# Windowed attention beside a ternary feed-forward layer: maxima as rows of the head stacks, masks in row groups of their own, three products a stack, two value buffers, new orders

## What is computed

```python
xn  = layernorm(x)
q, k, v = heads(xn @ Wq), heads(xn @ Wk), heads(xn @ Wv)     # 16 heads of 16
attn = softmax(q . k_window * 16**-0.5)     # a token sees itself and the 63 tokens before it
ctx = attn . v_window
h   = layernorm(gelu(xn @ ternary(W_fc).T), ln_w, ln_b)      # 1024 hidden features
out = x + ctx @ Wo + h @ ternary(W_proj).T
```

## Time and profile before

| what | value |
|---|---|
| median of three runs | 462.16 us |
| lowest and highest run | 457.6 and 462.68 us |
| the profiled execution, its own time | 454.42 us |
| its span, first to last instruction | 452.5 us |
| mean granted TensorE clock | 0.97 |

### The profile page before, as it was taken

One profiled execution on the slowest core, in us unless ns is written; L12 is line 12 of the kernel. 1 busy time (PEld: TensorE's weight loads), 2 busy tenths in 40 slices (PEclk: granted clock), 3 DMA queues, 4 the chain that ended last, 5 costly groups with the idle time before them and its releaser, 6 DMA issues.

```text
span 452.5 us, 13186 instructions
## 1 busy us (share of the span) xinstructions
PE 406.4 (90%) x5644; PEld 272.1 (60%) x5644; DVE 334.1 (74%) x693; ACT 309.1 (68%) x393; POOL 182.4 (40%) x112
## 2 busy tenths in 40 slices
PE   0396889799998999899998999999998999899894
PEld 0344554468646875578565874678465864677573
DVE  1885697559787887689767887689767975688664
ACT  2464278739677968877786758877786867796381
POOL 6200034245323644256305544255405731355572
PEclk9999799969999999999997999999999999999899
DMA  8759037800495046801691037801692029602001
GB/s 282 194 71 115 2 91 101 89 3 14 116 128 62 1 113 116 88 15 35 142 126 27 12 105 119 89 8 48 129 123 31 26 58 133 67 3 68 15 14 59
DMA packets 35226, 34.41 MB, mean 76 GB/s; under 512 B 5152, under 2 KB 33824, under 8 KB 35168
## 3 DMA queue, kind: packets, MB, share of 16 engines
q1 hardware_dynamic: 35168, 33.56, 44.7%
HBM read 7.35 MB, written 4.19 MB: 26 GB/s over the span
## 4 chain that ended last, share of the span: by engine, by line
PE 58%; DMA 14%; SPq 12%; DVE 7%; issue 4%; ACT 2%; POOL 2%; POOLq 0%
DMA k_stack<-qk_split 13%; SPq L324 11%; PE small L1114 8%; PE small L1103 7%; PE big L1093 6%; PE big L1021 6%; PE big L1081 5%; PE big L1033 4%; PE big L1066 4%; PE big L1060 4%; PE big L1086 3%; PE big L1047 3%; PE small L1130 2%; DMA x_in<-in_x 2%; PE big L1009 2%
## 5 line engine op out<-in xcount | busy, mean ns | idle before, releaser
L436 POOL TENSOR_TENSOR p_parts<-probs,p_parts 128x1024 f16<-128x1024 f32 x64 | 138.2, 2163 | 194.6 <-ACT p_parts L559 194.6
L558 ACT ACTIVATE probs<-big,exp_scale 128x1024 f32<-128x1024 f32 x64 | 71.4, 1115 | 53.3 <-PE big L1086 53.2
L738 DVE TENSOR_REDUCE negmax<-big 128x8 f32<-128x1024 f32 x64 | 78.1, 1222 | 23.0 <-PE big L1066 21.2
L559 ACT ACTIVATE p_parts<-big,exp_scale 128x1024 f16<-128x1024 f32 x64 | 71.3, 1114 | 0.0
L1103 PE MATMUL small<-proj_t,g_hi 128*128 128x256 f16 x256 | 60.8, 283 | 0.0
L1103 PE MATMUL small<-proj_t,g_lo 128*128 128x256 f16 x256 | 60.4, 282 | 0.0
L573 ACT ACTIVATE g_hi<-big,lnw_s 128x512 f16<-128x512 f32 x64 | 40.4, 689 | 25.5 <-PE big L1093 25.5
L1047 PE MATMUL big<-fc_t,xt_hi 128*128 128x512 f16 x128 | 48.7, 380 | 0.0
L1047 PE MATMUL big<-fc_t,xt_lo 128*128 128x512 f16 x128 | 48.5, 379 | 0.0
L732 DVE SCALAR_TENSOR_TENSOR g_lo<-big,lnw_s,g_hi 128x512 f16<-128x512 f32 x64 | 45.3, 739 | 2.4 <-ACT g_hi L573 2.1
L536 ACT ACTIVATE gel<-big 128x1024 f32<-128x1024 f32 x32 | 32.7, 1022 | 13.2 <-PE big L1047 12.8
(11 more groups left out here) (130 smaller groups left out, 786.4 us busy)
## 6 DMA issues: line engine op xcount, KB each, us to landing
q_stack<-qk_split SPq DMA_DIRECT2D x64, 128.0 KB, 4.3
k_stack<-qk_split SPq DMA_DIRECT2D x64, 128.0 KB, 7.3
x_in<-in_x SPq DMA_DIRECT2D x8, 512.0 KB, 4.8
out<-y_bufs SPq DMA_DIRECT2D x32, 128.0 KB, 1.7
v_odd<-v_even SPq DMA_DIRECT2D x16, 132.0 KB, 2.7
v_odd<-v_even SPq DMA_DIRECT2D x16, 99.0 KB, 2.2
y_bufs<-in_w_proj SPq DMA_DIRECT2D x1, 1024.0 KB, 5.5
gel<-in_w_fc SPq DMA_DIRECT2D x1, 1024.0 KB, 7.7
```

Of the source, the lines that this page charges most:

```text
L436: g.tensor_tensor(p_lo[:, j % PB], probs[:, j % PB], p_hi[:, j % PB], ALU.subtract).then_inc(*sig(p_lo_ready))
L558: s.activation(probs[:, j % PB].rearrange("p i (u q) -> p u i q", u=2), st, ACT.Exp, scale=exp_scale[:, 0:1]).then_inc(*sig(exp_ready))
L559: s.activation(p_hi[:, j % PB].rearrange("p i (u q) -> p u i q", u=2), st, ACT.Exp, scale=exp_scale[:, 0:1]).then_inc(*sig(p_hi_ready))
L738: v.tensor_reduce(negmax[:, j], slot[b, "sa", j][:].rearrange("p a (u k) -> p (a u) k", k=P), AX.X, ALU.max, negate=True).then_inc(*sig(ma ...
```

## The change

- Each stack has three products of 16 rows (lo·lo goes), so 12 DMAs a batch in place of 16. The two rows after them hold the split negated maxima, divided by 256, in `q_stack`, and 256 in `k_stack`. `fill_stacks` on DVE writes 256 over all of `k_stack` and zeros over its padding, ahead of `statistics(0)`; on POOL the zeros of `k_stack` go.
- `st` starts with two mask matmuls of 64 rows, one in each row group (`mask_k` is copied to partitions 64 to 127), its head matmuls have 50 rows, and those of `sa` 48. `shift`, `fill_shift` and `load_shift` go.
- `mt` is one job of four fp32 matmuls after all eight `sa`; `load_maxima` issues four DMAs of one row each.
- The values have two buffers; `v_upper` waits for the `pv` of two batches before.
- New lists for PE, ACT, DVE, POOL and SP: all eight `sa` of a batch stand ahead of its `gt`, `mt` and `st`, and x is loaded in the period in which its statistics are made. The first loads stand in another order.

```diff
-        v_even = sb("v_even", [P, 2, NT, NP, VC], fp16)
-        v_odd = sb("v_odd", [P, 2, NT, NP, VC], fp16)
+        v_even = sb("v_even", [P, 2, 2, NT, NP, VC], fp16)
+        v_odd = sb("v_odd", [P, 2, 2, NT, NP, VC], fp16)
...
-        negmax = sb("negmax", [P, NJ, NP], fp32)
-        mt = sb("mt", [4 * NP, 2, 2, P], bf16)
-        shift = sb("shift", [W + 2, NJ, NP * P], bf16)
+        negmax = sb("negmax", [P, NP, NJ], fp32)
+        mt = sb("mt", [P, 2, W], fp16)
...
-        PERIOD = [(-1, "pv", 6), (0, "gt", 3), (0, "mt", 0), (0, "v", 0), (-1, "pv", 7), (1, "xt", 0), (0, "sa", 4),
-                  (0, "proj", 0), (0, "st", 0), (1, "qk", 0), (-1, "ct", 1), (0, "st", 1), (1, "fc", 0), (0, "sa", 5),
-                  (-1, "wo", 1), (1, "qk", 1), (0, "sa", 6), (1, "fc", 1), (0, "pv", 0), (1, "fc", 2), (0, "sa", 7),
-                  (1, "fc", 3), (0, "st", 2), (0, "mt", 1), (0, "proj", 1), (0, "proj", 2), (0, "st", 3), (-1, "wo", 2),
-                  (1, "sa", 0), (0, "pv", 1), (1, "sa", 1), (0, "pv", 2), (0, "st", 4), (1, "sa", 2), (0, "st", 5),
-                  (0, "proj", 3), (0, "pv", 3), (1, "gt", 0), (0, "st", 6), (0, "pv", 4), (0, "ct", 0), (1, "sa", 3),
-                  (1, "gt", 1), (0, "st", 7), (0, "pv", 5), (-1, "wo", 3), (1, "gt", 2), (0, "wo", 0)]
-        ORDER = FIRST + [(p + ahead, kind, n) for p in range(NB + 1) for ahead, kind, n in PERIOD if 0 <= p + ahead < NB]
+        FIRST = [(0, "wmax", 0), (0, "spread", 0), (0, "sums", 0), (0, "xt", 0), (0, "wmax", 1), (0, "sums", 1),
+                 (0, "qk", 0), (0, "spread", 1), (0, "qk", 1), (0, "crow", 0), (0, "v", 0), (0, "fc", 0), (0, "fc", 1),
+                 (0, "csum", 0), (0, "sa", 0), (0, "sa", 1), (0, "sa", 2), (0, "fc", 2), (0, "sa", 3), (0, "fc", 3),
+                 (0, "sa", 4), (0, "sa", 5), (0, "sa", 6), (0, "sa", 7), (1, "xt", 0)]
+        PERIOD = [(0, "gt", 0), (0, "gt", 1), (0, "mt", 0), (-1, "pv", 5), (1, "qk", 0), (0, "gt", 2), (1, "qk", 1),
+                  (-1, "pv", 6), (-1, "ct", 0), (0, "gt", 3), (0, "st", 0), (-1, "pv", 7), (1, "v", 0), (0, "st", 1),
+                  (0, "st", 2), (-2, "wo", 3), (0, "proj", 0), (1, "fc", 0), (0, "pv", 0), (1, "fc", 1), (1, "sa", 0),
+                  (0, "st", 3), (0, "pv", 1), (1, "sa", 1), (0, "proj", 1), (0, "st", 4), (0, "pv", 2), (1, "sa", 2),
+                  (1, "fc", 2), (0, "pv", 3), (1, "sa", 3), (-1, "wo", 0), (1, "fc", 3), (0, "st", 5), (-1, "ct", 1),
+                  (0, "proj", 2), (1, "sa", 4), (0, "proj", 3), (0, "st", 6), (1, "sa", 5), (0, "pv", 4), (0, "st", 7),
+                  (-1, "wo", 1), (1, "sa", 6), (1, "sa", 7), (-1, "wo", 2), (2, "xt", 0)]
+        ORDER = FIRST + [(p + ahead, kind, n) for p in range(NB + 4) for ahead, kind, n in PERIOD if 0 <= p + ahead < NB]
...
-                    for other in range(2):
-                        a, c = (part, other) if s == 0 else (other, part)
-                        r = half * W + (a * 2 + c) * DH
+                    for product in (((0, 1), (2,)), ((0, 2), (1,)))[s][part]:
+                        r = half * W + product * DH
                         dst = (q_stack[r:r + DH, b % 2].rearrange("p i j q -> p i (j q)") if s == 0
...
-                sp.dma_start(v_odd[0:W, part, 1:NT], v_even[W:P, part, 0:NT - 1]).then_inc(*sig(v_shifted))
-                sp.dma_start(v_odd[W:P, part], v_even[0:W, part]).then_inc(*sig(v_shifted))
-            @per_batch
-            def load_shift(b, h):
-                wait(sp, b, mt_ready, h + 1)
+                sp.dma_start(v_odd[0:W, b % 2, part, 1:NT], v_even[W:P, b % 2, part, 0:NT - 1]).then_inc(*sig(v_shifted[b % 2]))
+                sp.dma_start(v_odd[W:P, b % 2, part], v_even[0:W, b % 2, part]).then_inc(*sig(v_shifted[b % 2]))
+            @per_batch
+            def load_maxima(b):
+                wait(sp, b, mt_ready, 1)
                 for c in range(2):
-                    sp.dma_start(shift[W + c:W + c + 1, h * HALF:(h + 1) * HALF, :], mt[:, h, c, :]).then_inc(
-                        *sig(shift_loaded[h]))
+                    for u in range(2):
+                        r = u * W + PARTS3 + c
+                        sp.dma_start(q_stack[r:r + 1, b % 2].rearrange("o i j q -> o (i j q)"),
+                                     mt[u * W:(u + 1) * W, c]).then_inc(*sig(maxima_loaded))
...
-            def fill_shift():
-                sp.wait_ge(onehot_ready, 1)
-                sp.dma_start(shift[0:W].rearrange("p j (u n) -> p (j u) n", u=2),
-                             onehot[0:W].rearrange("p i q -> p (i q)").unsqueeze(1).broadcast_to([W, 2 * NJ, NP * W])
-                             ).then_inc(shift_filled, 16)
             def copy_masks():
                 sp.wait_ge(masks_ready, 1)
                 sp.dma_start(mask_q[W:P], mask_q[0:W]).then_inc(masks_copied, 16)
-            load_ffn(1)
+                sp.dma_start(mask_k[W:P], mask_k[0:W]).then_inc(masks_copied, 16)
+            load_x(0)
             load_weights(0)
             load_ffn(0)
-            load_x(0)
+            load_weights(1)
             load_norm()
+            load_ffn(1)
             copy_masks()
...
+            for p in range(NB + 4):
+                store(p - 4, 2)
+                load_maxima(p - 2)
+                shift_values(p - 2, 1)
+                load_stack(p - 1, 0, 0)
+                load_stack(p - 1, 0, 1)
+                load_stack(p - 1, 1, 0)
+                load_stack(p - 1, 1, 1)
+                load_next_x(p - 1)
+                shift_values(p - 1, 0)
+                store(p - 4, 3)
+                store(p - 3, 0)
+                store(p - 3, 1)
...
-                if b > 0:
-                    wait(act, b - 1, pv_done, NJ)
+                if b > 1:
+                    wait(act, b - 2, pv_done, NJ)
                 else:
...
+            for p in range(NB + 4):
+                qk_upper(p + 1, 1)
+                context_upper(p - 1, 0)
+                gelu_upper(p, 6)
+                gelu_upper(p, 7)
+                exp(p, 0)
+                v_upper(p + 1)
+                exp(p, 1)
+                exp(p, 2)
+                gelu(p + 1, 0)
+                gelu(p + 1, 1)
+                exp(p, 3)
+                exp(p, 4)
+                gelu(p + 1, 2)
+                square(p + 1, 0)
+                gelu(p + 1, 3)
+                context_upper(p - 1, 1)
+                exp(p, 5)
+                exp(p, 6)
+                exp(p, 7)
+                square(p + 1, 1)
...
-                wait(dve, b, mt_done, h + 1)
-                row = slot[b, "mt", h][0:4 * NP, 0:P]
-                link(v.tensor_copy(mt[:, h, 0], row), b, max_step, h + 1)
-                v.tensor_tensor(mt[:, h, 1], row, mt[:, h, 0], ALU.subtract).then_inc(*sig(mt_ready))
+            def split_maxima(b):
+                wait(dve, b, mt_done, 1)
+                if b > 0:
+                    wait(dve, b - 1, maxima_loaded, 4)
+                row = slot[b, "mt", 0][:, 0:W]
+                link(v.tensor_scalar(mt[:, 0], row, 1.0 / MAX_UNIT, None, ALU.mult), b, max_step, 1)
+                v.scalar_tensor_tensor(out=mt[:, 1], in0=row, scalar=1.0 / MAX_UNIT, in1=mt[:, 0],
+                                       op0=ALU.mult, op1=ALU.subtract).then_inc(*sig(mt_ready))
...
+            def fill_stacks():
+                link_pre(v.memset(k_stack[:], MAX_UNIT))
+                v.memset(k_stack[:, :, :, 0:W], 0.0).then_inc(stacks_filled, 1)
...
+            fill_stacks()
+            statistics(0)
...
+            v_lower(1)
+            for p in range(NB + 4):
+                add_projection(p, 0)
+                scale_context(p, 0)
+                statistics(p + 2)
+                maximum(p + 1, 0)
+                scale_context(p, 1)
+                maximum(p + 1, 1)
+                add_projection(p, 1)
+                scale_context(p, 2)
+                maximum(p + 1, 2)
+                scale_context(p, 3)
+                add_attention(p - 1, 0)
+                normalize(p + 2)
+                maximum(p + 1, 3)
+                context_lower(p - 1, 1)
...
+                add_attention(p - 1, 1)
+                add_attention(p - 1, 2)
+                xt_lower(p + 2)
+                gelu_lower(p + 1, 0)
+                split_maxima(p + 1)
+                gelu_lower(p + 1, 1)
+                gelu_lower(p + 1, 2)
+                gelu_lower(p + 1, 3)
...
-                                rows = slice(u * W, (u + 1) * W)
-                                last = mm(ps[a * W:(a + 1) * W, u, i * P:(i + 1) * P], q_stack[rows, b % 2, 2 * i + a, n],
-                                          k_stack[rows, b % 2, 2 * i + a, n * W:n * W + P], start=False, stop=(i == 3))
+                                rows = slice(u * W, u * W + PARTS3)
+                                last = mm(ps[a * W:(a + 1) * W, u, i * P:(i + 1) * P], q_stack[rows, b % 2, 4 * a + i, n],
```

(39 more changed lines are left out.)

304 lines of the change are left out of this document (81 added, 223 removed).

## The result

The changed kernel takes 440.6 us (median of four runs, 440.4 to 444.5) where the kernel before takes 462.3 on the same chip (median of four, 457.6 to 462.7). Three of these four runs of before lie over 1.5% above its fastest execution (454.4, the profiled one) and count as slow, so the ratios here compare fast runs alone: 0.968, interval 0.963 to 0.973, where the medians would make 0.953. It is faster by 3%, where 8% were forecast. The profiled execution took 440.41 us with a span of 438.6.

A forecast was written before the change was run, and what follows sets the result against it. PE's list was taken to bound the periods, chains through other engines the start and end. Start 52.5, first period 43, six periods 284.4 and end 36 sum to 415.9 us; plus 1.9, times 1.017, gives 425 us, range 407 to 447.

The forecast's parts named there:

- The rule that I weighed there: On PE, a tiling mode change drains TensorE; `st` would save up to 0.1 us more a job, left to the range.
- Three products: Stack DMAs on SP's queue: 12 issues, not 16, so PE's wait for `k_stack`, 1.6 us a period, goes.
- the 1 us of slack: Before the first `sa`: PE's 14.4 us of jobs against 12.3 for the k part and 1 for ACT's readout.
- The start: Up to the first period: the fill takes 11 us, `statistics(0)` starts at 11 to 12, the period begins at 52.5 us.
- cold clock: PE's lowered clock, counted in the first period (43 us) and at the end (35, with it 36).
- The load of x: Behind the stack DMAs: DVE waits 0 to 3.7 us for x, costing PE 0 to 2.4 a period, taken as 0.5.
- Rival 1: DVE's list late in every period, by x or thin cover: 21 us more, 447 by the median; chance 0.16.
- The end: Last part: maxima 8 us, eight `exp` one after another 16.7, POOL 2.1, then 8.2: 35, with lowered clock 36 us.
- The median: Runs' median taken as 1.017 of the profiled execution, as before the change: 417.8 becomes 425 us.
- DVE's margins: DVE has 39 of 46 us a period; PSUM slots are often read with under half a microsecond spare: 0.5 us added.
- periods stay above 49 us: Sign that the forecast is wrong, shown by DVE waiting for x or PE for the maxima; periods forecast at 47.4 us.
- the start isn't shorter: Sign that the forecast is wrong: the start was forecast at 52.5 us, against 57.2 before.

The follow-up runs named there:

- before_three_pair: The kernel before with three products a stack, `st` masks each in its own row group, maxima left out of the exponent, its scale constant: 429.8 us, 0.949.
- x1_first_shift: The changed kernel with batch 1's x among the first loads and both halves of the values' copy issued together behind x: 427.1 us, 0.943.
- before_three: The kernel before with three products a stack (12 stack DMAs a batch, not 16) and nothing else of the change: 433.4 us, 0.952.
- x_early: The changed kernel with each load of x moved ahead of store 1 of the period before, not behind the stacks: 445.0 us, 0.978.
- light_pool: x1_first_shift with POOL forming the lower part of the probabilities for one head of eight only: 432.5 us, 0.945.
- gelu_copy: The changed kernel with ACT's gelu replaced by a plain copy, so no table loads in the periods: 449.2 us, 0.989.
- x1_first: The changed kernel with only the x of batch 1 loaded among the first loads: 437.8 us, 0.967.
- x1_first_one_product: x1_first with only the product of the two upper parts in the stacks, 4 DMAs a batch and not 12: 422.8 us, 0.935.

## Why the prediction was wrong

The time, 440.6 us, lies in the range but 15.6 above the forecast: the direction was right, and by the ratio less than half the gain came. PE's work a period (45.9 us), the mask pair (0.22 us a job in the old order, forecast 0.21), the table loads at nothing and `statistics` at 11 us were as forecast. The rule that I weighed there, that a change of the array's part drains TensorE, agrees with the rows, but `st` saved no such change: in the job of before_three_pair it moved to the front. By the steps that failed:

- **Three products: "Afterwards the k part starts with the second readout of `qk`", "The wait goes".** This step failed in the periods and is the main one, since its cause was in the diff. I counted the stacks' own issues from the readout on and left out the six that the new order puts right ahead of them, the maxima's four and two of `shift_values`; of the maxima I wrote that the stacks behind them need the readouts anyway. In the seven batches behind the first, the queue starts the k part 2.1 us on average after ACT's second readout, and 1.8 us of wait a period stay. Two issues less ahead of it gave 7 us (x1_first_shift). The rest of the sum was off too: PE's stretch between `qk` 1 and `sa` 0 is 13.2 us where I counted 14.4, and the k part lands 11.7 us after its start where I took 12.3. So the 1 us of slack lost 2.1 to the queue and 1.2 to that stretch, and got 0.6 back. In the old order the wait does go (before_three): nothing stands ahead there, and the readouts of the two `qk` are 7.1 us apart, not 3.5, so that the q part has a head start.
- **The start, 52.5 for 61.6 us.** The first `sa` is at 45.8 us and not at 42; the other 5 us come behind it. Two terms were missing there: the x of batch 1, whose load now stands behind the stacks of batch 0, with DVE's list waiting at 42 to 47 us ahead of the first maxima; and the lowered clock that follows (the "cold clock" of the prediction), which I had put into the first period alone. Ahead of the first `sa`, the two fills took 7.74 and 0.48 us (the second is issued as 512 words of 32 bits, not 1024 of 16), less than my 11 and than my estimate of 10.7, but DVE is then at `normalize` beside POOL's fills (3.10 us, alone 1.37), and PE waits 2.6 us for the absolute values of `w_proj`. With x, fill and absolute values repaired and the clock at 1.00 the first `mt` comes 10.2 us sooner (53.63 for 63.79); `normalize` still takes 3.11 us there.
- **The load of x, 0.5 us a period.** It cost nothing in the periods (x_early). x landed 9.3 us after its issue, near my upper bound of 9.65, and DVE waited 4.2 us a period, over my bound of 3.7, but caught up before its slot was needed. Rival 1, that this sets the period, is refuted; its place was the start.
- **The end, 36 for 42 us.** The `exp` don't follow one another: their starts are 2.0, 2.0, 2.4, 3.7, 4.4, 3.6 and 2.0 us apart, so that all eight take 21.9 us and not 16.7: 5.2 of the 6.0. From the fourth to the last start (411.85 to 425.42) PE is busy for 12.8 of 13.6 us: three jobs of `proj` at 1.85 us stand in its list between the last `st`, and I had left them out. DVE's additions, each longer beside POOL (mean 1.09 us in the span, 0.48 alone), add a little: a light POOL gives 2 us back (37.8 for 40.0). No run moved the `proj`, so this is read from the trace alone.
- **The median, 1.017 of the profiled execution.** The one profiled execution of before was faster than its runs; after the change the two agree (440.6 and 440.4). The factor came from the spread between executions of before and was no property of the kernel. This added 7.1 us to the forecast and hid as much of the error: the sum alone was 22.7 us off.
- **DVE's margins.** I took 39 us of DVE's work for granted. In the trace of before L774 already took 0.94 us on average where 0.48 is its length alone; DVE's load depends on when POOL works, and the new order moved that.

What I named as the test, "periods stay above 49 us", didn't come; the other, "the start isn't shorter", did: its end, the first `gt`, is at 61.6 us.

## What to carry to other kernels

Where a load or a copy is issued from a queue in order, follow what the queue issues in the 12 us ahead of it, not only its own data: at 0.64 us an issue, two copies that nobody waits for cost 1 us a period. Count the transfers from the first issue of the group, too: here they took 16 us however its issues lay. Do the parts of a large change one by one: here one part gave more than the whole (0.952 for 0.968), and the whole passed it, if at all, only after an x load and a copy had moved (0.943, with intervals that overlap). And when a kernel gets slower by less work on an engine that isn't the bound, look at what that engine now starts sooner.

## What the runs showed of the hardware

- **DVE and POOL can exclude each other.** A DVE operation with two operands in SBUF takes 0.48 us alone and 2.69 when POOL's 2.37 us began 0.04 us after it; the one ahead of it, L730 in light_pool, with an operand in PSUM, takes 0.48. The Trainium skill ("SBUF — State Buffer", Who interferes with whom) says that such a DVE instruction contends with a GpSimd one that reads SBUF, as both use one read port, and that whoever comes first holds it. That it contends agrees. But by the trace's starts DVE's instruction came first and still was the one that stood still, in 7 of 7 cases in light_pool and in 7 of 7 in gelu_copy. Which of the two was first to read SBUF, the trace doesn't show.
- **Change of the array's part.** From masks to heads 0.22 us where both use 64 rows by 128 columns, 0.24 in quarters, 0.32 where they differ, also when only the rows do (64 and 18). When the masks match their heads, the 0.1 us can move rather than go: in before_three_pair it stands ahead of the masks.
- **A fill on DVE** takes 0.84 us for 1000 elements, of 16 or of 32 bits (7.74 us for 9216, 3.90 for 4608).
- **Twelve DMAs of 128 KB** issued on one queue take 15.9 to 16.1 us on average from the first issue to the last landing, whether the issues follow one another (about 8 us for all twelve, x1_first) or have pauses (about 11 us, before_three); four take 6.3 to 7.1 (x1_first_one_product).
